# Condition row first in SyncE's queue, its sum first on VectorE, and the last quotient of the mixing in two token halves

## The reference

```python
tf = sigmoid(sum(time_emb, axis=-1))
decay = exp(-exp(w)) * (0.5 + 0.5 * tf)
ek = exp(minimum(k, 30));  ekv = ek * v
# forward and backward over tokens: a = a * decay + ekv, b = b * decay + ek
euk = exp(minimum(u + k, 30))
num = nf + nb - ekv + euk * v
den = df + db - ek + euk
out = sigmoid(r) * (num / maximum(den, 1e-8)) * (0.8 + 0.2 * tf)
```

## Time and profile before

| | us |
|---|---|
| median of 3 runs | 1457.3 |
| lowest and highest of them | 1453.5 to 1460.29 |
| the profiled execution, its own time | 1452.27 |
| its span, from first to last instruction | 1450.5 |
| outside the span | 1.8 |
| VectorE's first operation | 4.57 |
| first scan starts | 10.19 |
| last quotient ends, TensorE goes on | 47.51 |

### The profile page before, as it was taken

One profiled execution on the slowest core, in us unless ns is written; L12 is line 12 of the kernel. 1 busy time (PEld: TensorE's weight loads), 2 busy tenths in 40 slices (PEclk: granted clock), 3 DMA queues, 4 the chain that ended last, 5 costly groups with the idle time before them and its releaser, 6 DMA issues.

```text
span 1450.5 us, 22073 instructions
## 1 busy us (share of the span) xinstructions
PE 1365.4 (94%) x7888; PEld 767.7 (53%) x7888; DVE 1079.7 (74%) x2468; ACT 853.9 (59%) x1745; POOL 462.1 (32%) x375
## 2 busy tenths in 40 slices
PE   0879999999999999999999999988999999999998
PEld 0534754754664574575475476475444444444443
DVE  8898899889789889989988988955599675613000
ACT  4577677678578667767767857755533333212432
POOL 5151161161153135116116115215064343200432
PEclk9999999999999999999999999979999999999999
DMA  3120030030021022003003002102283444100220
GB/s 108 43 94 16 16 124 9 8 116 22 17 76 62 17 66 73 16 16 123 16 2 124 15 17 77 33 17 94 69 232 101 117 128 117 59 0 0 78 97 29
DMA packets 39092, 88.70 MB, mean 61 GB/s; under 512 B 5384, under 2 KB 25352, under 8 KB 37840
## 3 DMA queue, kind: packets, MB, share of 16 engines
q1 hardware_dynamic: 38704, 87.23, 19.5%
q10 hardware_dynamic: 288, 0.14, 0.0%
HBM read 84.77 MB, written 2.59 MB: 60 GB/s over the span
## 4 chain that ended last, share of the span: by engine, by line
PE 68%; DVE 18%; ACT 8%; issue 3%; DMA 2%; POOL 1%; DVEq 0%; ACTq 0%; SPq 0%; POOLq 0%
PE bank L512 13%; PE bank L1812 12%; PE bank L1790 11%; PE bank L1911 5%; DVE m L1179 5%; PE bank L611 4%; PE bank L626 4%; DVE m L1183 3%; PE bank L574 3%; PE bank L541 3%; DVE conv L1082 3%; PE bank L606 2%; PE bank L617 2%; PE bank L628 2%; ACT conv L834 2%
## 5 line engine op out<-in xcount | busy, mean ns | idle before, releaser
L1082 DVE SCALAR_TENSOR_TENSOR conv<-bank,taps,conv 128x510 f32<-128x510 f32 x366 | 270.4, 743 | 27.7 <-ACT conv L820 18.4
L512 PE MATMUL bank<-rT,wf 128*128 128x512 f32 x512 | 253.8, 611 | 6.9 <-DVE conv L1093 4.1
L1662 POOL TENSOR_TENSOR ffn_weighted<-ffn_relu,ffn_wide 128x512 f32<-128x512 f32 x96 | 128.7, 1374 | 299.9 <-DMA ffn_wide<-ffn_shares 148.0
L1812 PE MATMUL bank<-ffn_weighted,feat 128*128 128x512 f32 x400 | 186.8, 595 | 3.8 <-POOL ffn_weighted L1662 3.8
L1790 PE MATMUL bank<-rT,feat 128*128 128x512 f32 x400 | 187.4, 595 | 0.0
L1325 POOL TENSOR_TENSOR sq<-sq,qsq 128x512 f32<-128x512 f32 x64 | 82.9, 1296 | 270.3 <-ACT sq L1008 269.6
L1673 ACT ACTIVATE ffn_relu<-bank 128x512 f32<-128x512 f32 x100 | 59.6, 596 | 182.3 <-PE bank L1790 182.3
L512 PEld LDWEIGHTS bank<-rT,wf 128*128 128x128 f32 x512 | 89.5, 191 | 87.9 <-issue 73.7
L1812 PEld LDWEIGHTS bank<-ffn_weighted,feat 128*128 128x128 f32 x400 | 76.0, 190 | 100.1 <-issue 98.2
L1790 PEld LDWEIGHTS bank<-rT,feat 128*128 128x128 f32 x400 | 76.0, 191 | 93.9 <-issue 93.1
L574 PE MATMUL bank<-rT,wz 128*128 128x512 f32 x256 | 115.3, 604 | 8.9 <-DVE m L1183 6.1
(11 more groups left out here) (235 smaller groups left out, 2612.0 us busy)
## 6 DMA issues: line engine op xcount, KB each, us to landing
z<-decay_rows SPq DMA_DIRECT2D x64, 384.0 KB, 4.0
ffn_wide<-ffn_shares SPq DMA_DIRECT2D x64, 256.0 KB, 5.3
feat<-in_L_chunks_dram SPq DMA_DIRECT2D x25, 512.0 KB, 4.2
wf<-in_wf_dram SPq DMA_DIRECT2D x8, 1024.0 KB, 4.9
wz<-in_wz_dram SPq DMA_DIRECT2D x8, 512.0 KB, 3.6
wo<-in_wo_dram SPq DMA_DIRECT2D x8, 512.0 KB, 3.8
ffn_wide<-ffn_shares SPq DMA_DIRECT2D x8, 512.0 KB, 4.0
m<-in_fT_dram SPq DMA_DIRECT2D x2, 512.0 KB, 5.1
```

The lines of the kernel that those rows point to most:

```text
L512: ins = pe.matmul(banks[bank_of(p, n)][:], wf[:, c, ORDER[n // NH], :], rT[:, c, halves(n % NH)], start=(c == 0), stop=(c == CT - 1))
L1082: dve.scalar_tensor_tensor(acc[:, :, k:], src[:, :, 0:T - k], taps[:, ORDER[n // NH], KS - 1 - k:KS - k], acc[:, :, k:], ALU.mult, ALU.add ...
L1662: pool.tensor_tensor(hw[:, j, u, :], h2[:, j, u, :], wide[:, j, u // NH % BLOCKS, halves(u % NH)], ALU.mult).then_inc(weighted, 1)
L1812: last = pe.matmul(banks[4 + 2 * c + h][:], chunk[:, slot, CT + t, c * P:(c + 1) * P], of, start=start, stop=stop, skip_group_check=True)
```

## The change

The condition row is issued by SyncE ahead of everything else, and no longer by ScalarE. Its sum becomes VectorE's first operation, and `es` stands ahead of `into_bank(0)` on ScalarE. `least(1)` and `least_own(1)` move behind the first forward scan. The last quotient is computed for 512 tokens at a time, with `r_ready` raised after each half, and TensorE waits for each half by itself.

```diff
     def sync(sp):
+        sp.dma_start(cond, a["cond"].partition_broadcast(P)).then_inc(cond_in, 16)
         sp.dma_start(f[:, 0, :], a["fT"][0:P, :]).then_inc(f_in[0], 16)
...
         act.dma_start(wu[:], a["wu"]).then_inc(wu_in, 16)
-        act.dma_start(cond, a["cond"].partition_broadcast(P)).then_inc(cond_in, 16)
...
-        into_bank(0)
         act.wait_ge(tsum_ready, 1)
         act.activation(es, tsum, ACT.Exp, scale=-1.0).then_inc(decay_exps, 1)
+        into_bank(0)
         into_own(0)
...
+        def quotient_by_halves(c):
+            dve.wait_ge(rec_ready, 2 * c + 2)
+            step.need(step.n)
+            for h in range(NH):
+                x, y = df[:, c, halves(h)], db[:, c, halves(h)]
+                step(dve.tensor_tensor(x, x, y, ALU.mult))
+                step(dve.scalar_tensor_tensor(x, x, 2.0, y, ALU.subtract, ALU.mult))
+                dve.tensor_tensor(rT[:, c, halves(h)], nf[:, c, halves(h)], x, ALU.mult).then_inc(r_ready, 1)
...
+        dve.wait_ge(cond_in, 16)
+        dve.reduce_sum(tsum, cond, AX_X).then_inc(tsum_ready, 1)
         dve.wait_ge(f_in[0], 16)
         least(0)
         dve.wait_ge(wu_in, 16)
         least_own(0)
-        dve.wait_ge(cond_in, 16)
-        dve.reduce_sum(tsum, cond, AX_X).then_inc(tsum_ready, 1)
-        dve.wait_ge(f_in[1], 16)
-        least(1)
-        least_own(1)
         dve.wait_ge(decay_exps, 3)
...
         scan(0, df, ek, 1).then_inc(fwd_ready, 1)
+        dve.wait_ge(f_in[1], 16)
+        least(1)
+        least_own(1)
...
-        quotient(1)
+        quotient_by_halves(1)
...
-        pe.wait_ge(front["r_ready"], 2)
-        for n in range(2):
+        for n in range(NH):
+            pe.wait_ge(front["r_ready"], 2 + n)
             half(0, n, 1)
```

## The result

The changed kernel took 1462.91 us (median of 22 runs, 1457.15 to 1472.55), the kernel before 1457.28 (22 runs, 1448.98 to 1467.65). The ratio is 1.0046, with a 95% interval of 1.0028 to 1.0063: 6.7 us slower, between 4.1 and 9.2. It is a small loss, clear of noise, in place of the gain the edit looks like.

What follows compares the result with a forecast made beforehand. VectorE was taken to bound the front, the first 50 us, with shifts there carried into the total. Second scans 4.2 us later less 0.6 from the quotient gave +3.6 on 1457.3, so 1460.9 us; range 1454 to 1465.

Steps and rivals of the forecast that it cites:

- The bound of the front: First 50 us: VectorE is the bound, and a microsecond won or lost there is one in the total.
- The landing of tile 0: SyncE's queue: the row ahead makes tile 0 land 0.45 us later (0 to 0.67), at 5.02 for 4.57.
- rival 3: SyncE's queue: the row is slow by itself and delays tile 0 to 9.0; +7.6 us, median 1464.9, chance 0.07.
- The start of the scans: VectorE's front: without the wait, sum and tile 1 minima, first scans start near 7.12, some 2.1 us after tile 0.
- Where the minima land: VectorE behind the first scans: GpSimd holds tile 1's minima and `tout`; second scans start at 16.8 to 17.0, 4.2 us later.
- The turns: Shared SBUF ports: VectorE's two minima and `tout` alternate with GpSimd's three operations, one operation each.
- Rival 1: Moved minima: ports are no obstacle, minima cost 1.26 us where they are; -2.4 us, median 1454.9, chance 0.15.
- rival 2: Moved minima: VectorE is held once, then keeps its turn for all three; -0.9 us, median 1456.4, chance 0.10.
- rival 4: Moved minima: turns are taken, but `tout` slips in behind `least_own(1)`; +1.3 us, median 1458.6, chance 0.08.
- The last quotient: End of the mixing: halves start the convolution at 49.0 instead of 49.61, gain 0.6 us (0 to 1.2), limited by the taps.
- The sum: Whole kernel: +4.2 from the second scans less 0.6 from the quotient, +3.6 us, median 1460.9.

Runs made afterwards that it cites:

- the other two kernels with a late front: Changed kernel with the condition row back on ScalarE's queue, ratio 1.0043; kernel before with only tile 1's minima moved behind the first scans, ratio 1.0050.
- the run with GpSimd late: Changed kernel with GpSimd's first three operations of tile 0 kept back until `tout` is done; ratio 1.0014 [0.9985, 1.0044] to the kernel before.
- the halves alone: Kernel before with only the quotient of tile 1 in two halves; one execution without a ratio, convolution starting at 49.11 us instead of 49.61.

## Why the prediction was right, and where it was off

**The bound of the front.** Right. VectorE sets it, and its shift at 50 us is the kernel's within what can be measured: 5.63 us there, 4.8 in the last group, 4.5 at 1300 us, 6.7 [4.1, 9.2] in the ratio. In the other two kernels with a late front the last group is as late as the front or later (6.5 for 6.46, 7.3 for 5.34), so nothing takes the shift up as a rule.

**The landing of tile 0.** This step failed. I took 0.45 us, with an upper bound of 0.67 from the queue's busy time; it was 2.67. The queue's busy time was no bound: the row took 5.1 us from issue to landing at the head of SyncE's queue, and the same two loads on ScalarE's queue, with the row first, made that queue busy for 18.8% of the first 8 us and not 8.4%. The time to landing, 6.6 us for 128 KB when 512 KB landed in 3.8, was the better witness. I had its price as rival 3 and put it down as waiting behind the tiles. It was partly that: with nothing issued behind tile 0 on SyncE's queue, the row landed in 4.5. The larger part of tile 0's delay, which came with any load ahead of it, even one of 0.5 KB, had no row before and should have had a wider bound. The row also missed the 4.6 by which it had to be there for the sum to be hidden; at 5.83 the sum stayed hidden only because tile 0 was later still.

**The start of the scans.** Right in its parts: 9.33 - 7.24 = 2.09 us after tile 0 for the 2.10 of the working, and GpSimd's first operation at 10.99 - 7.24 = 3.75, exactly the number worked out.

**Where the minima land.** Right, and it decided the sign. The second scans came 18.79 - 7.24 = 11.55 us after tile 0, where the working had 11.8 to 12.0. The turns were taken one by one, as it said. Rival 1 (no obstacle), rival 2 (held once) and rival 4 (`tout` slips in) are refuted by the rows of after and by the run with GpSimd late. The Trainium skill's rule (SBUF — State Buffer, Who interferes with whom) is that the one that issues first holds the shared ports for its whole instruction. The trace agrees: the minimum issued at 11.67, into an operation of GpSimd that ran from 10.99 to 13.33, ended at 13.88. GpSimd's next was recorded from 13.41, when that minimum had waited since 11.67, and came second. The turns fit that rule, since the one that waits has issued first.

**The last quotient.** Expected 0.6, measured 0.47 in the changed kernel and 0.50 with the halves alone. The taps were the limit, as worked out: 1.45 without them.

**The sum.** Forecast +3.6, and the front gave +5.63. The gap of 2.0 us is 2.2 more at the landing, 0.35 less at the turns (11.55 for 11.9) and 0.13 less gained at the quotient. The 6.7 of the ratio is another 1.1 above that, which lies inside its interval. The ratio's lower end of 4.1 lies above my sum: the sign and the mechanism were right, the size was not. That the range held the 1462.9 is in part luck, since only rival 3, at 0.07, had stretched it beyond the forecast.

## What to carry to other kernels

Before moving a VectorE copy or tensor-scalar operation, look at what GpSimd does at the time it will run then, not at its place in the code: three operations worth 1.6 us were held until 7 us of GpSimd's work were through. Such a loss shows as longer durations and not as waits, so compare the same line's durations between traces. Putting a small load ahead of a large one that is waited for isn't free, as 0.5 KB ahead of tile 0 cost 2.5 us: time to landing is the number to read, and not the bytes. A row broadcast to all partitions took twice as long to land as the same bytes in different rows. And before believing the span of one execution, look at the granted clock of its stretches: half of the 9.5 us between the two profiles was a clock dip 1290 us behind the change. When one step is cut in pieces to start its follower early, check everything else the follower waits for.

## What the runs showed of the hardware

- VectorE's tensor-scalar operations and GpSimd's tensor-tensor operations on SBUF ran one at a time, and with work ready on both they took turns, each operation recorded with its wait: 2.21, 2.83, 2.31 us on VectorE for 0.68, 0.75 and 0.16, and 2.67, 2.79 on GpSimd for 2.35. An operation of 4 elements waited as long as one of 1024 (2.15 us, against 1.53 and 2.08). Scans that read one operand from PSUM kept their 2.42 us for four beside GpSimd.
- A DMA of 128 KB that reads one row of 1 KB 128 times landed 5.0 to 5.3 us after issue at the head of SyncE's queue; one of 128 different rows landed in 2.4.
- 512 KB landed 3.8 to 4.2 us after issue as the first load of SyncE's queue, 5.3 to 6.2 as the second (5.9 behind 0.5 KB), and 4.3 as the second with nothing issued behind it. As the first, but with the broadcast row first on ScalarE's queue, it took 5.8.
- The same 12 matmuls took 5.40 us at a granted clock of 1.00 and 8.25 with 0.50 for part of them; the fall to 0.50 came in one of two executions that did the same work ahead of it.
